# Six buffers for the output weights, and four smaller changes of order, in the first attention of a decoder layer

## What is computed

```python
def bitnet_linear(x, weight, scale_param):
    s = jnp.maximum(jnp.mean(jnp.abs(weight), axis=1), 1e-08)
    binary_w = jnp.sign(weight / s[:, None])
    y = jnp.einsum('bsi,oi->bso', x, binary_w)
    y = y * (s * scale_param)[None, None, :]
    ...
x = x + attention(layernorm(x), q_weight, q_scale, k_weight, k_scale, v_weight, v_scale, o_weight, o_scale)
```

## Time and profile before

| | us |
|---|---|
| median of 3 runs | 926.94 |
| lowest and highest | 922.7, 929.55 |
| the profiled execution, whole | 931.98 |
| its span, from first to last instruction | 930.2 |
| its granted TensorE clock, mean share of full | 0.927 |

### The profile page before, as it was taken

One profiled execution on the slowest core, in us unless ns is written; L12 is line 12 of the kernel. 1 busy time (PEld: TensorE's weight loads), 2 busy tenths in 40 slices (PEclk: granted clock), 3 DMA queues, 4 the chain that ended last, 5 costly groups with the idle time before them and its releaser, 6 DMA issues.

```text
span 930.2 us, 15527 instructions
## 1 busy us (share of the span) xinstructions
PE 815.3 (88%) x5786; PEld 426.1 (46%) x5786; DVE 653.5 (70%) x1390; ACT 435.6 (47%) x860; POOL 319.6 (34%) x305
## 2 busy tenths in 40 slices
PE   3899899999999999899974789886689999999987
PEld 3565343333333333466652323234556556656643
DVE  6875477888898886577774768425377687778771
ACT  4475516777777777033442357533323333424410
POOL 1100005767767778010100135342222422423310
PEclk9999998999999999999987678657799999999998
DMA  8574722222223131202128131110001011011011
GB/s 328 206 251 145 204 82 83 77 81 90 68 89 99 59 124 41 90 13 82 53 83 295 40 111 43 48 40 22 1 1 24 24 46 23 23 45 34 1 34 57
DMA packets 75772, 75.81 MB, mean 81 GB/s; under 512 B 37509, under 2 KB 63893, under 8 KB 75062
## 3 DMA queue, kind: packets, MB, share of 16 engines
q1 hardware_dynamic: 75142, 68.77, 23.9%
q10 hardware_dynamic: 560, 6.12, 1.7%
HBM read 53.56 MB, written 21.04 MB: 80 GB/s over the span
## 4 chain that ended last, share of the span: by engine, by line
PE 60%; DVE 14%; ACT 8%; issue 6%; DMA 5%; SPq 3%; POOL 3%; POOLq 0%; DVEq 0%; ACTq 0%; PEldq 0%
PE psum L2066 6%; PE psum L1699 5%; PE psum L1785 5%; PE psum L1836 4%; PE psum L2027 4%; PE psum L1893 4%; PE psum L1825 4%; DVE m_neg L1317 3%; PE psum L1900 3%; PE psum L1846 3%; PE psum L2088 3%; PE psum L1993 3%; PE psum L1971 2%; DMA qk_scr<-hi_st 2%; SPq L552 2%
## 5 line engine op out<-in xcount | busy, mean ns | idle before, releaser
L1317 DVE TENSOR_REDUCE m_neg<-psum 128x1 f32<-128x512 f32 x256 | 166.0, 683 | 29.5 <-PE psum L1785 27.5
L942 ACT ACTIVATE region_x<-psum 128x512 f32<-128x512 f32 x256 | 142.9, 596 | 57.3 <-PE psum L1825 55.6
L697 POOL TENSOR_TENSOR region_p<-region_x 128x2048 f32<-128x2048 f32 x32 | 145.1, 4534 | 40.3 <-ACT region_x L942 26.8
L1785 PE MATMUL psum<-ops 96*128 96x512 f16 x256 | 98.4, 392 | 9.1 <-DVE m_neg L1317 8.3
L1825 PE MATMUL psum<-ops 98*128 98x512 f16 x256 | 97.5, 388 | 0.9 <-ACT region_x L942 0.8
L1699 PE MATMUL psum<-region_x,region_w 128*128 128x512 f16 x320 | 73.3, 384 | 1.2 <-ACT region_x L855 1.2
L1836 PE MATMUL psum<-region_x,v_g 128*32 128x512 f32 x512 | 67.8, 604 | 0.0
L1785 PEld LDWEIGHTS psum<-ops 96*128 96x128 f16 x256 | 25.2, 98 | 90.2 <-DVE m_neg L1317 71.2
L1893 PE MATMUL psum<-sign_o_all,region_a 128*128 128x512 f16 x256 | 58.5, 379 | 3.9 <-DVE region_p L1400 2.8
L2066 PE MATMUL psum<-region_a,c_o 128*128 128x512 f16 x256 | 60.4, 391 | 0.0
L1082 ACT ACTIVATE region_p<-psum 128x512 f32<-128x512 f32 (+2 forms) x96 | 39.2, 463 | 38.7 <-PE psum L1982 38.4
(11 more groups left out here) (253 smaller groups left out, 1616.3 us busy)
## 6 DMA issues: line engine op xcount, KB each, us to landing
ops<-q_scr SPq DMA_DIRECT2D x48, 128.0 KB, 2.6
region_a<-in_x SPq DMA_DIRECT2D x8, 512.0 KB, 8.7
region_a<-in_w_q SPq DMA_DIRECT2D x8, 512.0 KB, 7.1
region_w<-in_w_o SPq DMA_DIRECT2D x8, 512.0 KB, 4.1
region_w<-in_kern SPq DMA_DIRECT2D x16, 256.0 KB, 3.0
kern_scr<-region_w SPq DMA_DIRECT2D x32, 128.0 KB, 1.9
region_p<-in_x SPq DMA_DIRECT2D x8, 512.0 KB, 3.6
region_a<-kern_scr ACTq DMA_DIRECT2D x1, 4096.0 KB
```

The source lines that it names most:

```text
L697: pool.tensor_tensor(pair_sum[:, n], prob_a[:, 2 * n], prob_a[:, 2 * n + 1], ALU.add).then_inc(pair_ready, 1)
L942: act.activation(prob_a[:, kt, j, :], psum[:, (0, 4, 5)[(16 * i + n) % 3], :], ACT.Exp, scale=A_SCALE).then_inc(p_ready, 1)
L1317: dve.tensor_reduce(m_neg[:, i % 3, n:n + 1], psum[:, 1 + (16 * i + n) % 3, :], AX_X, ALU.max, negate=True).then_inc(s_max, 1)
L1785: pe.matmul(psum[:, 1 + (16 * i + n) % 3, :], qa_op[u][0:A_MAX, j, qt * P:(qt + 1) * P], k_op[u][0:A_MAX, :], start=True, stop=True).then_ ...
```

## The change

1. `w_o` gets six buffers: the two in `region_w` and four in `region_a`, where the query chunks 0, 1, 4 and 5 lay (the late stages of the queries use the other four). Behind the read of `rows`, SP waits for the last `abs_query` and issues the reads of chunks 2 to 5 one behind the other; 4 waits till 2 has landed, 5 till 3. Chunks 6 and 7 go to the buffers of 0 and 1, behind `store_q(1)` and `store_q(2)`.
2. The sines move from behind `sign_out(7)` to behind the tenth `q_hi` (i = 9).
3. `turn_x` of tiles 0 to 3 no longer waits for `xT_free`.
4. In VectorE's list `value_rows(0)` moves from behind `turned_lo(6)` to behind `turned_lo(5)`, and `value_rows(1)` from behind `turned_lo(7)` to ahead of it.

```diff
-        o_in = [region_w[:, u * D:(u + 1) * D] for u in range(2)]
+        o_in = [region_w[:, u * D:(u + 1) * D] for u in range(2)] + [region_a[:, u * D:(u + 1) * D] for u in (0, 1, 4, 5)]
...
             def load_o(c):
-                if c >= 2:
-                    sp.wait_ge(signs_done, 20 + 2 * (c - 1))
-                    sp.wait_ge(abs_summed, 14 + c - 2)
+                if c >= 6:
+                    sp.wait_ge(signs_done, 20 + 2 * (c - 5))
+                    sp.wait_ge(abs_summed, 14 + max(c - 6, 1))
                 wait_weights(sp, KC - 2 + c if c < 2 else c - 2, o=c >= 2)
-                sp.dma_start(o_in[c % 2], d["w_o"][:, c, :]).then_inc(w_loaded[c % 2], 16)
+                sp.dma_start(o_in[c % 6], d["w_o"][:, c, :]).then_inc(w_loaded[c % 2], 16)
...
             sp.dma_start(rows[:], d["rows"]).then_inc(w2_loaded, 16)
+            sp.wait_ge(abs_summed, 14)
+            for c in range(2, 6):
+                load_o(c)
...
             for i in range(Q_EARLY):
                 store_q(i)
-                if i + 2 < KC:
-                    load_o(i + 2)
+                if i in (1, 2):
+                    load_o(i + 5)
...
-            act.wait_ge(trig_done, 1)
-            for k in range(2):
-                act.activation(trig[:, k], trig_r[:, k], ACT.Sin).then_inc(trig_done, 1)
-            act.wait_ge(trig_done, 2)
-            act.activation(trig[:, 2], trig[:, 0], ACT.Copy, scale=-1.0).then_inc(trig_done, 1)
+            def sines():
+                act.wait_ge(trig_done, 1)
+                for k in range(2):
+                    act.activation(trig[:, k], trig_r[:, k], ACT.Sin).then_inc(trig_done, 1)
+                act.wait_ge(trig_done, 2)
+                act.activation(trig[:, 2], trig[:, 0], ACT.Copy, scale=-1.0).then_inc(trig_done, 1)
...
             for i in range(Q_EARLY, NI):
                 q_hi(i)
+                if i == Q_EARLY + 1:
+                    sines()
...
             turned_lo(5)
+            value_rows(0)
             k_lo(1)
             turned_lo(6)
-            value_rows(0)
+            value_rows(1)
             turned_lo(7)
-            value_rows(1)
             abs_query(1)
...
             def turn_x(i):
                 pe.wait_ge(xn_ready, i + 1)
-                pe.wait_ge(xT_free, 2 * i + 2)
+                if i >= 4:
+                    pe.wait_ge(xT_free, 2 * i + 2)
```

More of the change, by code:

```diff
@@ L865, in sign_out @@
                 wait_weights(act, c, o=True)
-                act.activation(sign_o[:, c, :], o_in[c % 2], ACT.Sign).then_inc(signs_done, 1)
+                act.activation(sign_o[:, c, :], o_in[c % 6], ACT.Sign).then_inc(signs_done, 1)
                 act.wait_ge(signs_done, 20 + 2 * c + 1)
-                act.activation(o_in[c % 2] if c else abs_o, o_in[c % 2], ACT.Abs).then_inc(signs_done, 1)
+                act.activation(o_in[c % 6] if c else abs_o, o_in[c % 6], ACT.Abs).then_inc(signs_done, 1)
             def k_hi(n):
@@ L1226, in abs_out @@
                     dve.wait_ge(abs_summed, 14 + c - 1)
-                dve.tensor_tensor(abs_o, o_in[c % 2], abs_o, ALU.add).then_inc(abs_summed, 1)
+                dve.tensor_tensor(abs_o, o_in[c % 6], abs_o, ALU.add).then_inc(abs_summed, 1)
             def k_lo(n):
```

## The result

The changed kernel took 919.59 us in the median against 927.67 for the kernel before, run beside it: a ratio of 0.9923, interval 0.9900 to 0.9945. The forecast was 918.7, 0.9 us off. The profiled execution took 919.7 us (span 917.9) against 931.98: 12.3 us less, 4 more than the medians differ, so not all that the two traces differ by belongs to the change. Up to the first exponential they differ by 8.4 us. The first attention gives 2.3 more, the first out projection takes 1.3 back, and what follows gives 3.0.

A forecast was written before the change was run, and what follows sets the result against it. TensorE, busy 88% of the span, was taken as the bound, with gains only at the ends of its rigid bar. 2.1 + 1.0 + 3.5 + 1.6 = 8.2 us off 926.94 gave 918.7; range 914.5 to 923.5 for 8 in 10.

The forecast's parts named there:

- Turns, 2.1 us: First four turns of x tiles without a wait: VectorE ends tile 3's low half sooner, gain 2.1 us.
- the bar: TensorE's block from 45 to 105 us, busy throughout at full clock; only its two ends can give; start 3.1 us sooner.
- the front end: Work before 43.58 us, where TensorE waits for VectorE four times; turns and value rows give 3.1 us.
- Value rows, 1.0: Third value product at 43.58 us no longer waits for the first `value_rows`: gain 1.0 us, bounds 0.4 and 1.03.
- Six buffers, 3.5, and 0.7 left: Reads of `w_o` no longer delay `sign_out`: gain 3.5 us of the 4.18 us stall before the fourth score, 0.7 stays.
- Clock, 1.6: Granted clock after the stall before the fourth score goes to the upper level: gain 1.6 us, bounds 0 and 1.6.
- Sines, 0: Sines moved into ScalarE's 4.49 us wait for TensorE behind the tenth query: cost 0, no gain by itself.
- The shift should travel to the end: Behind 110 us all waits are relative, so the whole 8.2 us gain should reach the end.
- Rivals 3 and 4: Clock at 495 to 690 us: 3, better, 914.8 us, chance 0.22; 4, worse, over 1% slower, chance 0.03.
- The price of the clock in rivals 3 and 4: At 495 to 690 us, 0.01 of mean granted clock over 140.6 us of busy time costs about 1.9 us.
- The sign named there: Forecast is wrong if 495 to 690 us, shifted, lasts over 2 us more or less.

The follow-up runs named there:

- experiment 2: Only the four turns without the wait for `xT_free`, on the kernel before; one execution took 929.55 us.
- experiments 1 and 8: 1: six buffers alone on the kernel before, median 918.58 us, ratio 0.9918. 8: whole change with the sines in the old place, median 919.85 us, ratio 0.9907.
- experiment 4: Whole change without the six buffers (turns, value rows and sines), against the kernel before: median 923.16 us, ratio 0.9953.
- experiment 7: Whole change and six buffers alone run side by side, repeated: medians 919.59, 920.02, 918.91 us against 918.58, 917.89, 918.93 us.

## Why the prediction was right, point by point

- *Turns, 2.1 us:* right, with its reason: VectorE's low halves set the end (20.39, worked out as 20.4). 2.1 by themselves at the bar's start, experiment 2. The working counts four waits of TensorE for VectorE ahead of the bar; its list shows six (8.49, 16.94, 26.57, 32.78, 41.48, 43.58), which changes nothing in the sum.
- *Value rows, 1.0:* right, and no later wait took it back. Bar forecast at 40.4, measured at 40.31. By the means of all traces (43.2 in five, 39.8 in seven) the front end gives 3.4, for 3.1 in the sum.
- *Six buffers, 3.5, and 0.7 left:* right (3.5 and 0.66). The train's size was wrong: the working had all four reads in by 76, but the fourth was issued only at 76.0, and a read of the train landed 6.5 us behind its issue (median), not 5.4. It cost nothing, because the chunks and the store's buffer are wanted much later. The Trainium skill, *DMA: Bandwidth & Descriptors*, section Queues, rings and completion order, has SP's descriptors (the pieces of a transfer) consumed in ring order on each DMA engine. No run here put the stores ahead of the train, so what that order costs isn't shown. It cost TensorE nothing that the trace shows: no sign waits for its chunk, and from the fifth to the eighth query tile, where the stores' buffers are wanted again, `q_hi` stands 0.73 us each time for TensorE and not for a buffer.
- *Clock, 1.6:* right for the pair compared (1.6), but a fixed value was the wrong form: of six traces with the stall, four show 1.4 to 1.7 and two 2.9.
- *Sines, 0:* right, experiments 1 and 8.
- Forecast for the end of the queries 8.2, measured 8.4.
- *"The shift should travel to the end":* this step failed. With the six buffers alone 5.1 us are gained at the first exponential and 8 to 9 in the medians; with the whole change 8.4 and 6 to 8. The 3.1 us of the front end don't show when these two are compared (0.7 us slower, give or take 0.9), although the front end shows by itself (experiment 4: 0.9953, 0.9930 to 0.9975). The waits are relative, as the working said; the clock is not. Rivals 3 and 4 had the clock's share as luck around a mean that stays; experiment 7 says that the mean itself may differ from kernel to kernel, and why is open. That the total came out within 1 us of the forecast is thus in part luck: the six buffers gave more than their 5.1 and the front end, on top of them, less than its 3.1.
- *The price of the clock in rivals 3 and 4*, 1.9 us for 0.01 of the mean: not borne out. The stretch that the working watches, 495 to 690 us, is taken here from the second attention's first score to the dense layer's first matmul. In it the mean fell from 0.74 to 0.69, and it took 213.9 us instead of 215.0. The sign named there, 2 us more or less in this stretch, can't tell anything either: two traces of the kernel before differ by 5.6 us in it, three of the whole change by up to 6.7.

## What to carry to other kernels

A rigid block of matmuls has two ends: look for what starts it and for the first stall behind it, and cost only these. A buffer that is one too few shows as a chain transfer, sign, sum, maximum on three engines, and its price here was the stall and the low clock behind it. Where the clock changes later on, a gain of 3 us early can't be taken as 3 us in the time: compare variants by a place ahead of that stretch, measured from an earlier common place, and the whole by many executions.

## What the runs showed that was not expected

- Behind idle times of 4.2 to 4.9 us TensorE's granted clock was at its lower level (1.2 GHz) for 3.4 us in four traces and 6.8 in two, and nearly the same idle time (4.41 and 4.18) brought 2.9 and 1.6 us of loss.
- It fell with shorter stops as well, and not each time: behind the same 2.83 us of idle time in the first out projection in 9 of 14 traces; at 147 us, where the stops ahead are 0.86 and 0.25 us, in one.
- Four reads of 512 KB, with two waits among them, held SP's queue for 7.84 to 9.20 us in three traces of the whole change and 7.98 to 8.57 in three of the six buffers alone.
